# A graph kernel whose row gathers have 125 or 128 rows: another choice of tiles for each

## What is computed

```python
edge_index = jnp.stack([src, dst])
x = _layernorm(x + _L0_gnn_ref(x, edge_attr_2, ..., edge_index), axis=-1)
x = _layernorm(x + _L1_gnn_ref(x, edge_weight, edge_attr_3, edge_index, ...), axis=-1)
```

## Time and profile before

| | |
|---|---|
| median of 3 runs | 9764.92 us (9756.39 to 9769.67) |
| the profiled execution | 9772.5 us |
| its span, first to last instruction | 9770.7 us |
| mean granted TensorE clock | 0.83 |
| busy share of the span | PE 71%, DVE 61%, ACT 28%, POOL 70% |

### The profile page before, as it was taken

The page is one execution under the profiler, slowest core; times in us unless marked ns, Lnnn a source line. Parts: engine busy times, 40 slices in busy tenths (PEclk is TensorE's granted clock), DMA queues, the critical chain, the costliest instruction groups (busy, mean ns, idle before and its releaser), DMA issues. The chain is left out here.

```text
span 9770.7 us, 126395 instructions
## 1 busy us (share of the span) xinstructions
PE 6954.9 (71%) x31138; PEld 3523.2 (36%) x31138; DVE 5975.6 (61%) x15302; ACT 2780.0 (28%) x6973; POOL 6861.8 (70%) x6409
## 2 busy tenths in 40 slices
PE   4555566665655555455678888888888888888888
PEld 2222222222222222222334444444444444444444
DVE  4334334343443434333478888888888888888888
ACT  1000000000000000000154444444444444444443
POOL 6666666666666666666577777777777777777776
PEclk7666666667776666666699999999999999999999
DMA  1111111101111111111022222222222222222222
GB/s 28 13 13 13 13 13 13 14 13 14 13 13 13 13 13 13 13 13 13 13 70 54 55 54 55 54 55 54 55 54 55 54 55 54 55 54 55 54 55 50
DMA packets 738237, 336.46 MB, mean 34 GB/s; under 512 B 620559, under 2 KB 688074, under 8 KB 737964
## 3 DMA queue, kind: packets, MB, share of 16 engines
q0 software_dynamic: 307200, 209.96, 10.8%
q10 hardware_dynamic: 20480, 102.42, 4.0%
q1 hardware_dynamic: 410537, 23.86, 2.9%
HBM read 325.86 MB, written 6.40 MB: 34 GB/s over the span
## 5 line engine op out<-in xcount | busy, mean ns | idle before, releaser
L601 PE MATMUL sums_all<-shared 125*64 125x289 f32 x6400 | 2142.5, 510 | 1704.0 <-issue 1690.7
L172 POOL DMA_INDIRECT rows<-table_dram,idx_a x1920 | 2295.8, 1196 | 654.4 <-issue 650.4
L172 POOL DMA_INDIRECT rows<-in_x,idx_a x1920 | 1816.9, 946 | 1106.3 <-issue 567.8
L601 PEld LDWEIGHTS sums_all<-shared 125*64 125x64 f32 x6400 | 925.4, 165 | 2702.1 <-issue 2410.3
L172 POOL DMA_INDIRECT rows<-table_dram,idx_b x1280 | 1537.0, 1201 | 390.1 <-issue 382.2
L910 PE MATMUL sums_ps<-prods,hot 125*64 125x272 f32 x12800 | 1630.7, 401 | 186.5 <-issue 157.6
L470 DVE TENSOR_TENSOR own_ps<-factors 125x45 f32<-125x45 f32 x640 | 135.6, 212 | 2660.0 <-remote 2252.7
L172 POOL DMA_INDIRECT rows<-in_x,idx_b x1280 | 1211.2, 946 | 703.4 <-issue 372.9
L688 ACT ACTIVATE flat<-sums_all 64x289 f32<-64x289 f32 x640 | 261.5, 409 | 4360.8 <-remote 3293.0
L900 PE MATMUL radial_x<-w2p,hidden 128*125 128x384 f32 x3840 | 1410.1, 503 | 34.8 <-ACT hidden L865 33.6
L900 PE MATMUL radial_y<-w2p,hidden 128*125 128x384 f32 x2560 | 1028.3, 525 | 444.4 <-DVE prods L1016 331.6
(11 more groups left out here) (151 smaller groups left out, 5448.0 us busy)
## 6 DMA issues: line engine op xcount, KB each, us to landing
dist_ab<-in_edge_weight ACTq DMA_DIRECT2D x128, 468.8 KB
dist_ab<-in_edge_weight ACTq DMA_DIRECT2D x128, 312.5 KB
rows<-in_x,idx_a POOLq DMA_INDIRECT x1920
rows<-table_dram,idx_a POOLq DMA_INDIRECT x1920
rows<-in_x,idx_b POOLq DMA_INDIRECT x1280
rows<-table_dram,idx_b POOLq DMA_INDIRECT x1280
vec_s<-in_edge_attr SPq DMA_DIRECT2D x129, 36.6 KB
idx_a<-in_src SPq DMA_DIRECT2D x257, 7.3 KB
```

The lines of the kernel that those rows point to most:

```text
L172: pool.indirect_dma_start(out=rows[u][0:n, j, 0:width], out_offset=None, in_=table, in_offset=bass.IndirectOffsetOnAxis(ap=idx[u // 3][0:n ...
L601: last = pe.matmul(sums_ps[s][:, 0:K + 1], hot[s][:, j, :], spread[s][:, j, :], start=(j == 0), stop=(j == G - 1))
```

## The change

The two tuples are set anew. In loop 1 the gathers of tiles 1 and 3 of each unit keep 128 rows, and those of tiles 0, 2 and 4 get 125. In loop 2 the gather of tile 2 gets 128 rows, and the others keep 125. Nothing else is changed.

```diff
-FULL_0, FULL_1 = (0, 1, 2, 3, 4), ()
+FULL_0, FULL_1 = (1, 3), (2,)
```

## The result

The changed kernel takes 9694.65 us (median of 4 runs, 9678.58 to 9710.77), the kernel before 9763.65 us on the same chip (median of 4, 9756.39 to 9769.67): a ratio of 0.9935, 95% interval 0.9922 to 0.9948. It is 69 us faster; 508 us had been forecast, and the time lies above the range (8780 to 9620).

What follows compares the result with a forecast made beforehand. POOL's gathers were taken to bound both loops, with loop 1 also pausing because 128-row gathers held up PE. 9772.5 - 346 (loop 1) - 161 (loop 2) = 9265.5, less 7.6 for the median: 9258 us, range 8780 to 9620.

Steps and rivals of the forecast that it cites:

- What bounds the kernel: Both loops: POOL's gathers set the pace; in loop 1 128-row gathers delay PE's increments, 6.5 us of POOL wait a turn.
- The price of a narrow 125-row gather: Loop 1: a 32-column gather of 125 rows costs 1.502 us start to start, adding 478 us of issue.
- cheap-gather rival: Loop 1: narrow 125-row gathers cost 1.251 us like 128-row ones, and the standstill goes; 8780 us, chance 0.20.
- The rule of the Trainium skill, DMA: Bandwidth & Descriptors: Gathers: the largest number up to 16 dividing the row count is how many DMA engines share it, 16 or 5.
- I take the wait as gone: Loop 1: POOL's wait of 6.5 us a turn vanishes once 125-row gathers separate the 128-row ones; -823 us.
- the standstill lasts as long as POOL has 128-row gathers to issue: Loop 1: PE, DVE and ACT stand until POOL runs out of 128-row gathers; 125-row ones don't hold them up.
- the 4450 forecast: Loop 1 as a whole: 4450 us after the change, from turns of 35.04 instead of 37.76 us, -346 us.
- -0.251 x 640 = -161 us: Loop 2: 640 gathers go to 128 rows and each saves 0.251 us, with POOL still setting the pace; -161 us.
- this rival, one 128-row gather in a unit holding PE between DVE's steps: Loop 2: each 128-row gather holds PE's increments for up to 1.25 us; +397 us, 9816 us, chance 0.06.
- A fixed turn: Loop 1: a PE, ACT and DVE chain independent of POOL fixes 37.76 us; only loop 2 gains; 9604 us, chance 0.10.
- The standstill stays: Loop 1: any gather holds PE's increments, so the 6.5 us wait stays and it grows 478 us; 10082 us, chance 0.14.
- The rule beside it: Every tile should have 128 partitions; by it loop 1 could only lose, at the price of "The standstill stays".

Runs made afterwards that it cites:

- e3: All gathers of both loops with 125 rows, against the kernel before (9759.35 us on that chip): 9819.6 us, ratio 1.0065.
- e4: All gathers of both loops with 128 rows, against the kernel before (9759.35 us on that chip): 10854.96 us, ratio 1.1134.
- e9: The changed kernel itself, against the kernel before on another chip (8926.84 us there): 9351.30 us, ratio 1.0477.
- e2: Only loop 2's half of the change (tile 2 with 128 rows; loop 1 all 128), against the kernel before (9759.35 us): 9942.34 us, ratio 1.0201.
- e1: Only loop 1's half of the change (tiles 1 and 3 with 128 rows; loop 2 all 125), against the kernel before (9759.35 us): 9665.96 us, ratio 0.9908.
- the first four experiments: e1, e2, e3 and e4, each the kernel before with another choice of rows, on one chip where the kernel before took 9759.35 us.
- e10: All gathers of both loops with 128 rows, against the kernel before on another chip (8926.84 us there): 8465.52 us, ratio 0.9483.
- e6: 126 rows in each gather of loop 1 in place of 128, against the kernel before on another chip (8919.14 us there): 9136.08 us, ratio 1.0241.

## Why the prediction was wrong

**What bounds the kernel.** Right: POOL sets both loops, and the pause of loop 1 came from PE's late increments. e3 shows that they are gone when no gather has 128 rows, e4 that 128-row gathers bring them into loop 2, and the chips without the hold that the pause was worth 840 us.

**The price of a narrow 125-row gather**, 1.502 us start to start: right. It is 1.513, against 1.257 with 128 rows, for rows of 128 and of 384 B. The packets are not the price: the gather queue of the changed kernel moved 286720 packets. At 64 for each of the 2560 wide 125-row gathers, 122880 are left for the other 3840, 32 each on average. With 125 rows everywhere (e3) it moved 307200; less 64 for each of 3200 wide gathers, 102400 are left, 32 for each narrow one: the narrow 125-row gathers leave as many as 128-row ones and still take 1.21 us. This refutes the cheap-gather rival (8780 us). I had argued the price from the packets, which I took to follow the row count and not the width; they follow the width too, so the price came out right by an argument that does not hold. The rule of the Trainium skill, DMA: Bandwidth & Descriptors, "Why a DMA increments its semaphore by 16 and not by 1", agrees with the packets: by it a narrow 125-row gather puts one packet of 3200 B on each of 5 engines, and of the 32 packets from 2507 to 2508.5 us in after 5 are of 2 KB or more.

**"I take the wait as gone"**: this is the step that failed. I reasoned that a 125-row gather after each one or two of 128 would let PE run free. In the trace of after PE crawls through both kinds alike, 1.40 us a matmul, and a turn still has 1.2 us beyond its issue. That the standstill lasts as long as POOL has 128-row gathers to issue did not hold either: POOL pauses 41 times, but ACT comes out of 359 "remote" waits. The same kernel without the hold (e9) runs loop 1 from 39.71 to 4523.85, 4484.1 us, which is within 34 us of the 4450 forecast; on the result's chip the loop missed it by 185, of which 151 are the hold (4635.1 - 4484.1). Of the 437 us by which the forecast was off (9694.65 - 9258), these 185 are the smaller part.

**"-0.251 x 640 = -161 us" in loop 2**: the larger part, 252 of the 437 us. The price itself was right (0.96 us), and without the hold loop 2 takes 4697.7 us in e9 against 4799 to 4854 with 125 rows. With the hold it takes 4898.0. So 200 of the 252 us are the hold, which the sum had put at nothing here; the other 52 are there without it too, and 2560 x (1214 - 1198) ns = 41 us of them are the longer 125-row gathers of this program. I had worked out this rival, one 128-row gather in a unit holding PE between DVE's steps, and given it 0.06; it came true at about a quarter of its price, +92 instead of +397 us (in e2, +179). The trace of before had the reason to weigh it more: its loop 2 showed that 125 rows do no harm, and nothing at all of how it stands 128. I used the absence of the hold in a loop without its cause as evidence of robustness. It wasn't: loop 2 hands over between PE and DVE five times a turn, and its DVE, at 6.18 us a unit, has only 1.08 us to spare in the new unit of 7.26.

**A fixed turn** (9604 us) comes nearest to the measured time, but by luck: its turn of 37.76 us did not stay (36.50), and its gain in loop 2 is a loss. **The standstill stays** (10082 us) is refuted by e3 as it was meant, "by any gather"; in part it does stay. The rule beside it, to tile to 128 partitions always (the Trainium skill, Trainium Kernel Development and Optimization, Best Practices), when taken for the gathers, holds without the hold, where 128 rows everywhere is 5.2% faster than before, and fails with it, where they cost 11%.

**The two halves do not add up.** e1 gives -93 us and e2 +183, together +90, but the change gives -69. In e2 loop 2 is 87 us longer than in the changed kernel with the same choice of tiles, and I have no experiment that says why. Programs differ in the duration of the same 125-row gather too (1196 ns in before, 1210 in e1), so loop 2 can shift by 49 us with nothing changed in it; but between e2 and the changed kernel this goes the other way, 1193 ns in e2 against 1214.

With the hold, e1 is the fastest of the six kernels run there, 9666 us; without it, of those tried, 128 rows everywhere, 8466 us.

## What to carry to other kernels

That a stage does not show a stall is evidence only for the conditions it runs under; when a change brings the suspected cause into that stage, price it there as a loss and not only as the saved issue time. Where a gain is the end of a stall, ask for the trace in which the stall is absent and its cause half as strong, since a milder stall may stay. And a stall may be there on one chip and not on the next: run the kernel before on another one before choosing by it, as here the choice of rows that was slowest with the stall is the fastest without it.

## What the runs showed of the hardware

**The hold was there on some chips and not on others.** The kernel before took 9743 to 9775 us on the chip of the result and on that of the first four experiments, and 8917 to 8931 us on five others. The six chips of the experiments were each used once, and all runs with the hold came before those without it, so it isn't shown that it belongs to the chip and not to something that changed in time. With the hold, PE's matmuls start late, in stretches, and DVE and ACT resume from waits named "remote", in a loop that has gathers of 128 rows; with 125 rows in all they don't (e3). Its size is 840 us of this kernel, and 2389 us of the one with 128 rows everywhere (10855 against 8466). The mechanism isn't known: I tried neither another engine as the issuer nor, on such a chip, 126 rows. TensorE's granted clock in loop 2 was 0.89 in e4 and 1.00 in e10 (5200 to 8200 us), that is, always at its 2.4 GHz in e10 and for part of the time at 1.2 in e4, where PE stood idle in each standstill. Whether that idleness is all that lowered it wasn't tried.

**POOL's time for an indirect gather goes by which row count it has, not by bytes or packets**: means of 944 to 977 ns for 128 rows, 995 to 997 for 126, and 1192 to 1219 for 125, each with 0.30 us behind it; for 128 and 125 rows the same with rows of 128 and of 384 B. Three rows less cost about 0.25 us more, one row less than 126 about 0.2. Between 126 and 125 rows the number of equal parts, of at most 16, that the rows fall into goes from 14 to 5; that this makes the difference was expected (e6) and fits the three row counts, but isn't shown.
